# ScalarE's rounding of the transposed second-norm rows, before and behind the exponentials of its step

## What is computed

```
x = _ln(src) * (1.0 + scale) + shift
scores = einsum('bhqd,bhkd->bhqk', q / sqrt(16), k) + attention_bias
scores = where(src_mask, -inf, scores)
probs = softmax(scores, axis=-1)
x = x + (einsum('bhqk,bhkd->bhqd', probs, v) @ Wo + bo)
h = _ln(x) * g2 + beta2
ff = _gelu2(h @ W1 + b1) @ W2 + b2
return x + ff
```

## Time and profile before

| | us |
|---|---|
| median of 3 runs | 1372.82 (1371.82 to 1374.18) |
| the profiled execution | 1370.21 |
| its span, first to last instruction | 1368.4 |
| TensorE busy | 1237.3 (90%) |
| VectorE busy | 974.0 (71%) |
| ScalarE busy | 901.0 (66%) |
| GpSimd busy | 702.8 (51%) |
| mean granted TensorE clock | 0.978 |

### The profile page before, as it was taken

One profiled execution on the slowest core, in us unless ns is written; L12 is line 12 of the kernel. 1 busy time (PEld: TensorE's weight loads), 2 busy tenths in 40 slices (PEclk: granted clock), 3 DMA queues, 4 the chain that ended last, 5 costly groups with the idle time before them and its releaser, 6 DMA issues.

```text
span 1368.4 us, 34309 instructions
## 1 busy us (share of the span) xinstructions
PE 1237.3 (90%) x9799; PEld 1141.1 (83%) x9799; DVE 974.0 (71%) x2767; ACT 901.0 (66%) x2319; POOL 702.8 (51%) x612
## 2 busy tenths in 40 slices
PE   4887599999999999994579999999999999999996
PEld 3776599999999999993458888888888888888885
DVE  5676687988788888763478677676666766777662
ACT  3343577787787778771357777677677767777772
POOL 2677386877787777774324433434333343333322
PEclk9999999999999999996799999999999999999998
DMA  5785311212111221213877666667666676656620
GB/s 182 241 271 193 115 51 49 58 58 58 59 58 45 53 60 56 59 43 106 270 225 220 198 213 200 213 204 229 196 209 188 212 228 196 210 184 211 216 86 16
DMA packets 184660, 203.13 MB, mean 148 GB/s; under 512 B 18209, under 2 KB 172657, under 8 KB 184529
## 3 DMA queue, kind: packets, MB, share of 16 engines
q1 hardware_dynamic: 169232, 161.65, 38.3%
q10 hardware_dynamic: 9120, 23.33, 5.4%
q0 software_dynamic: 6176, 16.79, 3.7%
HBM read 160.01 MB, written 41.71 MB: 147 GB/s over the span
## 4 chain that ended last, share of the span: by engine, by line
PE 42%; issue 4%; ACT 3%; DVE 3%; DMA 1%; ACTq 1%; POOL 0%; another core or an unknown queue 0%; POOLq 0%; DVEq 0%
PE ps_p L1384 8%; PE ps_s L1370 4%; PE ps_ctx L1400 4%; PE ps_s L1372 4%; PE ps_out L1496 3%; PE ps_q L1496 3%; PE ps_q L1482 2%; PE ps_k L1482 2%; PE ps_q L1449 2%; PE ps_out L1440 2%; ACT bias L1278 2%; PE ps_q L1457 2%; PE ps_k L1449 2%; PE ps_q L1486 1%; PE ps_k L1486 1%
## 5 line engine op out<-in xcount | busy, mean ns | idle before, releaser
L1278 ACT ACTIVATE bias<-bias,neg_max 128x256 f32<-128x256 f32 x512 | 255.1, 501 | 85.2 <-DVE neg_max L1606 83.2
L348 POOL TENSOR_TENSOR w_lo<-w,w_hi 128x512 fp32r<-128x512 f32 x156 | 242.1, 1572 | 0.0
L1606 DVE CUSTOM_DVE_ANT_0 bias<-ps_s,bias 128x256 f32<-128x256 f32 x512 | 194.4, 417 | 35.5 <-PE ps_s L1372 19.3
L751 DVE TENSOR_TENSOR w_lo<-w,w_hi 128x512 fp32r<-128x512 f32 x156 | 150.9, 1006 | 68.1 <-ACT w_hi L429 66.4
L550 PE MATMUL ps_y<-w_hi,hidT_hi 128*128 128x256 f32 x624 | 180.2, 289 | 1.9 <-DVE token_rows L765 1.9
L537 PE MATMUL ps_h<-htokT_hi,w_hi 128*128 128x256 f32 x624 | 178.3, 286 | 3.2 <-DVE htokT_lo L756 3.2
L1384 PE MATMUL ps_p<-const,bias 128*128 128x128 f32 x1024 | 156.9, 276 | 23.7 <-ACT bias L1278 22.3
L537 PE MATMUL ps_h<-htokT_lo,w_hi 128*128 128x256 f32 x624 | 178.0, 285 | 0.0
L537 PE MATMUL ps_h<-htokT_hi,w_lo 128*128 128x256 f32 x624 | 178.0, 285 | 0.0
L550 PE MATMUL ps_y<-w_hi,hidT_lo 128*128 128x256 f32 x624 | 177.0, 284 | 0.0
L550 PE MATMUL ps_y<-w_lo,hidT_hi 128*128 128x256 f32 x624 | 177.0, 284 | 0.0
(11 more groups left out here) (281 smaller groups left out, 3521.3 us busy)
## 6 DMA issues: line engine op xcount, KB each, us to landing
bias<-bias_dram SPq DMA_DIRECT2D x128, 512.0 KB, 4.8
w<-w_dram ACTq DMA_DIRECT2D x32, 512.0 KB
xin<-dispatch SPq DMA_DIRECT2D x39, 256.0 KB, 2.9
expert_out<-token_rows SPq DMA_DIRECT2D x39, 256.0 KB, 2.2
q_stack<-q_hi_rows SPq DMA_DIRECT2D x64, 128.0 KB, 2.9
q_stack<-q_lo_rows SPq DMA_DIRECT2D x64, 128.0 KB, 3.0
k_stack<-k_hi_rows SPq DMA_DIRECT2D x60, 128.0 KB, 2.9
k_stack<-k_lo_rows SPq DMA_DIRECT2D x60, 128.0 KB, 2.9
```

The costliest lines, as they stand in the source:

```text
L348: pool.tensor_tensor(w2_part["lo"][:, k, :], w2_piece(e, k), w2_part["hi"][:, k, :].bitcast(F32), ALU.subtract).then_inc(sem("w2_split"), 1)
L751: dve.tensor_tensor(w1_part["lo"][:, k, :], w1_piece(e, k), w1_part["hi"][:, k, :].bitcast(F32), ALU.subtract).then_inc(sem("w1_split"), 1)
L1278: act.activation(head_rows(h, j), head_rows(h, j), ACT.Exp, scale=-1.0, bias=neg_max[par][:, h, j:j + 1], accum_out=total[par][:, h, j:j + ...
L1606: dve.tensor_tensor_reduce(head_rows(h, j), ps_s[h % 2][:, j * T:(j + 1) * T], head_rows(h, j), -1.0, LARGEST, ALU.add, ALU.min, neg_max[p ...
```

## The change

In ScalarE's `step`, `take_hT(n - 1)` of step 6 moves from ahead of `exponentials` to behind it. In step 6 these are the exponentials of head 7. Nothing else is changed: no instruction is added, removed or resized, no wait changes, and the other engines' queues are the same. The move acts where both stand in the code: in entries 1 to 15 (15 times). Behind entry 15 there is one more `take_hT`, with no exponentials beside it.

```
                 if h == 3 and exists(n + 1):
                     upper(n + 1, "k", ps_k, vec[:, K_B:K_B + C])
+                if exists(ahead):
+                    exponentials(ahead, head, par if head else 1 - par)
                 if h == 6 and exists(n - 1):
                     take_hT(n - 1)
-                if exists(ahead):
-                    exponentials(ahead, head, par if head else 1 - par)
                 if h == 1 and exists(n + 1):
```

## The result

| | before | after |
|---|---|---|
| median of 6 runs | 1373.50 (1371.41 to 1375.94) | 1365.37 (1360.86 to 1365.67) |
| the profiled execution | 1370.21 | 1365.67 |
| its span | 1368.4 | 1363.9 |

The ratio of the runs is 0.9931, with a 95% interval of 0.9912 to 0.9950: the change makes the kernel faster, by 8.1 us in the medians. The median is 2.0 above the forecast of 1363.4. The two profiled executions are only 4.5 apart, though, where the sum of the prediction had 9.4. By their traces these 4.5 are 0.7 ahead of the first `turn_h`, in the part that the change doesn't touch, 5.3 from the first `turn_h` to the fifteenth, and 1.5 lost behind it. The 5.3 in the middle are what the experiments are about.

What follows compares the result with a forecast made beforehand. TensorE bounds the kernel, waiting 19.4 us for exponentials. Gains of 9.5 + 0.5 - 0.2 - 0.4 = 9.4 us take the profiled 1370.21 to 1360.8; the median, 2.6 above, becomes 1363.4 us, range 1360.2 to 1368.5.

Steps and rivals of the forecast that it cites:

- The bound: The 15 bodies, 720 to 1340 us: TensorE, busy 596.9 of 620 us, sets the time; only its waits can be won.
- the wait of 1.27 at head 7: TensorE's transposes of head 7, entry 6: they wait for exponentials queued behind take_hT on ScalarE; the wait goes.
- rival of banks: Head 7's transposes wait for ps_p1 to be emptied of head 5, so nothing moves: 1372.8 us; chance 0.03.
- `take_hT` 0.05 late in entry 6: ScalarE: take_hT starts at 941.38 instead of 941.33; split_hT and minimum(8) on VectorE each follow 0.05 later.
- (a): Entry 6, feed_up(0): its fifth product needs hT_lo, seen at about 942.83; a new TensorE wait of about 0.2.
- (b): Entry 6: from the hT_lo product to turn_probs(8) TensorE has 1.41 us of work, so it gets there at 944.24.
- (c): Entry 6: turn_probs(8) waits 0.4 us for head 8's exponentials, going from 945.40 to 944.64; 0.76 of 1.27 won.
- Marks in the profile: Signs foretold: wait for exponentials 7 to 9 us, 0.4 idle before head 7's, waits 0.2 at hT_lo, 0.4 at head 8.
- Does the 0.76 last?: Behind turn_probs(8): TensorE's feeders move up with it, only the DMA queue does not; entry 3 gives back 0.4.
- Given back at the turn of the entry: Something TensorE does not drive holds steps 0 to 5, so entries start at their old times: 1372.8 us; chance 0.07.
- Bias pair 7: Its DMA holds minimum(14) and becomes the bound, each entry giving back 0.4: 1368.2 us; chance 0.15.
- Slower: Late minimum of head 7 makes its exponentials hold up take_hT and head 8: at worst 1377.0 us; chance 0.05.

Runs made afterwards that it cites:

- the late gather: Both kernels, GpSimd's gather made to wait until all heads of the entry before were weighed: before 1382.55 us, after 1381.88 us.
- the gather early: Gather issued a body ahead, at the end of GpSimd's body: kernel before 1402.53, after 1405.10, after with split_hT behind minimum(8) 1398.89 us.
- `split_hT` behind: Kernel after, split_hT moved behind minimum(8), here with ordinary transfers of fixed rows for the indirect ones: 1352.21 us; with the indirect ones kept, 1360.44.

## Why the prediction was right, and where it was off

- **The bound, and the wait of 1.27 at head 7.** Right, in every entry: the order on ScalarE was the cause. With it the rival of banks falls. The Trainium skill, Perfetto Trace Analysis, Optimization Strategy, reads a gap that repeats as a possible want of buffers; the 0.71 to 0.83 us of gain in entries 2 to 14, with the same banks, decide for the releaser that the row named.
- **`take_hT` 0.05 late in entry 6, 0 to 0.13 in entries 2 to 14.** Measured 0.06, and 0.00 to 0.13.
- **(a), (b), (c): 0.76 won at head 8 in entry 6, 0.73 in the mean.** Measured 0.77, and 0.71 to 0.83. Entry 15 won 0.61 for 0.5. Entry 1 was foretold 0.2 worse: its `take_hT` was 0.51 late for 0.94 and it won 0.35 at head 8 in the first trace, and it lost 0.07 in the second.
- **Marks in the profile.** The wait for exponentials is 6.7 us for a foretold 7 to 9; 0.44 of idle stands ahead of `exponentials(7)` for 0.4; the wait for `hT_lo` is 0.18 for 0.2. At head 8's transposes the row says 0.21 where 0.4 was foretold, though they start 3.94 behind `turn_h` for a foretold 3.95: TensorE's work ahead of them took some 0.2 longer than the 1.41 of the prediction.
- **"Does the 0.76 last?"** This is the step that was off; that the time still fell into the range owes something to its width. The step says that everything that feeds TensorE is released by TensorE's own work and so moves up with it. `take_ctx` is released by TensorE's `weigh`, but it hears of it up to 2.45 us late, in most rounds when GpSimd's last issue of the gather ends or 0.6 to 0.9 behind that, and the row `ACT ctxT L1307 <- remote`, 27.1 us in 11 waits before, had been passed over because its engine is not the bound. The view that showed no gap from 943.03 to 965.00 ended 10 us short of that place. Of the 0.73 in the mean a round keeps 0.60 to 0.68 with the hold alike. Over 14 rounds that makes some 1.3 us of the 2.0 by which the median missed. The other 0.7 is the base: with three more runs the median of the kernel before went from 1372.82 to 1373.50.
- **The profiled pair.** 5.3 us in 14 rounds where 8.9 were foretold. 3.5 of this is the hold by the reckoning above, which the profile before had short by chance. Behind the fifteenth `turn_h` 0.5 was foretold and 1.5 lost, 1.6 of it by the clock at the last projection, where the profile before was lucky again. The prediction took one execution for the kernel. That its sum, made from this execution, came within 2.0 of the median is in part luck.
- **Given back at the turn of the entry.** The place of this rival is right, its mechanism (held by something that TensorE does not drive) half right, its size wrong: it was priced as all or nothing, with a chance of 0.07, and costs about a tenth of a us in a round, and 0.7 where a short hold turns into a long one.
- **Bias pair 7.** It does not bound most entries. The loss comes in single rounds: 43.66, 42.97, 43.26 and 42.06 are all round 4, each with a minimum that waited 1.1 to 2.3 us for the pair and a round 0.9 to 1.8 too long. The price of 0.4 for one entry was too low, the count of entries too high.
- **Slower.** Its mechanism was met in the kernel after in entry 1 alone, as foretold, and was made in the other entries by the late gather: 0.67 late, 0.6 of gain gone.

## What to carry to other kernels

Before a gain is carried to the end, follow the chain through a whole period of the loop, not to the end of the gap-free stretch, and look on the engines that are not the bound for waits whose releaser had long been done. Two executions of one kernel can differ by more than the change is worth (1368.59 to 1377.32 for the kernel before on one chip; the untouched part ahead of the first `turn_h` alone took 726.5 to 733.0 in the 14 traces), so set a round against one with the same waits in it, and let medians of several runs give the size. And a place freed on one engine shows the next one: the chain over `split_hT`, 0.35 in each body, was in the sum as a cost before it was tried as a gain.

## What the runs showed of the hardware

**Indirect transfers of GpSimd delay what other engines wait for.** While GpSimd issues four of them (1.0 us each and 0.3 between), releases from TensorE late in the issuing reached ScalarE up to 2.45 us late and VectorE up to 2.35. Wherever the four stood, a delay stood. With the gather at its place, the held instruction starts in rounds 1 to 11 at the end of the fourth issue (within 0.04) or 0.6 to 0.9 behind it, and in round 12 mostly 0.7 ahead of that end; with the gather behind `weigh(3)` it is 0.8 to 1.05 behind it. Not every release in that time is held: with the gather behind `weigh(3)`, `k_hi` follows TensorE by 0.05 us, 1.2 us into the issuing, and VectorE's minimum releases ScalarE within 0.03, 3.6 us into it. Four ordinary transfers of the same size from the same queue (2.23 us together), through before the release, delayed `take_ctx` by nothing, and neither did two indirect ones that were through before it. What carries the delay, and what chooses between the two starts, no run here tells.

**At the loop's turn VectorE stands still for 2.4 to 2.9 us.** This is so in rounds 4, 6, 8 and 10, in which the hardware loop of two entries jumps back, ahead of its first instruction of the new pass, for nothing that the profile names (with the gather early 2.5 to 3.2). From the kernel after:

```profile
962.06 0.41 DVE L1692 TENSOR_TENSOR x3b<-ps_q,x3b 128x256 f32<-128x256 f32 x1
965.01 0.42 DVE L1606 CUSTOM_DVE_ANT_0 bias<-ps_s,bias 128x256 f32<-128x256 f32 x1 [2.53 <-issue]
```

It is in the traces with the hold and in those without. Where the hold is away, even rounds are still longer than odd ones: by 0.35 to 0.67 us before (42.13 to 42.45 for 41.78) and by 0.3 after (41.42 for 41.10), so the change wins more in them, but by 0.5 to 0.6 again with `split_hT` behind (41.19 to 41.32 for 40.69). That the jump is the cause is argued from its place; a loop of another length wasn't run.
